# Cross attention: the maximum subtracted inside the transposed score product, the clip between product and exponential

## What is computed

```python
scale = D ** (-0.5)
q = (query @ Wq + bq).reshape(B, Nq, H, D).transpose(0, 2, 1, 3)
k = (key_value @ Wk + bk).reshape(B, Nkv, H, D).transpose(0, 2, 1, 3)
v = (key_value @ Wv + bv).reshape(B, Nkv, H, D).transpose(0, 2, 1, 3)
attn = jnp.einsum('bhqd,bhkd->bhqk', q, k) * scale
attn = jnp.clip(attn, -CLAMP, CLAMP)          # CLAMP = 10000
attn = jax.nn.softmax(attn, axis=-1)
attn = jnp.where(jnp.any(jnp.isnan(attn)), jnp.asarray(1.0 / Nkv, attn.dtype), attn)
x = jnp.einsum('bhqk,bhkd->bqhd', attn, v).reshape(B, Nq, Cq)
return x @ Wo + bo
```

## Time and profile before

| what | value |
|---|---|
| three runs | 860.56, 868.16, 869.66 us |
| median | 868.16 us |
| span of the profiled execution | 862.7 us |
| TensorE matmul busy | 727.4 us, 84% |
| VectorE busy | 639.6 us, 74% |
| ScalarE busy | 408.4 us, 47% |
| GpSimd busy | 198.2 us, 23% |
| mean granted TensorE clock | 0.931 of full speed |

### The profile page before, as it was taken

One profiled execution on the slowest core, in us unless ns is written; L12 is line 12 of the kernel. 1 busy time (PEld: TensorE's weight loads), 2 busy tenths in 40 slices (PEclk: granted clock), 3 DMA queues, 4 the chain that ended last, 5 costly groups with the idle time before them and its releaser, 6 DMA issues. The chain is left out here.

```text
span 862.7 us, 26300 instructions
## 1 busy us (share of the span) xinstructions
PE 727.4 (84%) x10112; PEld 545.5 (63%) x10112; DVE 639.6 (74%) x1802; ACT 408.4 (47%) x777; POOL 198.2 (23%) x317
## 2 busy tenths in 40 slices
PE   3468898888888889889999477887759999999997
PEld 2245565555556777667787245665547888888886
DVE  7568877787868989888996577887665766666653
ACT  3123223322235656656655365665635555554553
POOL 3333222232534212330200553342011110011100
PEclk9569989998898999999999599999998999999999
DMA  4000000140034221122200000000000000000000
GB/s 103 9 22 13 23 21 21 33 88 18 24 99 100 82 78 50 53 66 79 81 15 14 4 2 5 5 4 4 5 3 2 13 13 0 12 12 12 12 13 13
DMA packets 33082, 26.43 MB, mean 31 GB/s; under 512 B 9740, under 2 KB 29912, under 8 KB 32984
## 3 DMA queue, kind: packets, MB, share of 16 engines
q1 hardware_dynamic: 29944, 24.07, 10.5%
q10 hardware_dynamic: 3040, 0.98, 0.5%
HBM read 13.51 MB, written 7.34 MB: 24 GB/s over the span
## 5 line engine op out<-in xcount | busy, mean ns | idle before, releaser
L1931 PEld LDWEIGHTS bank<-w2r,hme 128*128 128x128 f32 x1024 | 132.2, 191 | 15.6 <-ACT hme L1876 1.4
L1931 PE MATMUL bank<-w2r,hme 128*128 128x128 f32 x1024 | 135.5, 276 | 0.0
L1876 ACT ACTIVATE hme<-bank,b 128x512 f32<-128x512 f32 x128 | 86.5, 687 | 96.3 <-PE bank L97 96.3
L984 ACT ACTIVATE P<-bank 128x512 f32<-128x512 f32 x128 | 76.6, 598 | 76.2 <-PE bank L1130 75.0
L1900 DVE SCALAR_TENSOR_TENSOR Xq<-bank,wgte,Xq 128x128 f32 (+1 forms) x256 | 72.1, 344 | 51.1 <-PE bank L1931 38.3
L1056 DVE TENSOR_SCALAR bank<-bank 128x512 f32<-128x512 f32 x128 | 89.6, 700 | 15.2 <-PE bank L1121 14.4
L1064 DVE TENSOR_REDUCE mx<-bank 128x4 f32<-128x512 f32 x128 | 87.1, 681 | 1.4 <-PE bank L1104 1.3
L500 ACT ACTIVATE w2r<-bank 128x512 f32<-128x512 f32 x40 | 23.9, 597 | 114.5 <-PE bank L814 82.8
L1130 PE MATMUL bank<-mT,negsel 128*128 128x128 f16 x512 | 51.0, 223 | 13.9 <-DVE bank L1056 12.6
L95 PE MATMUL bank<-xTe,w 128*128 (+1 forms) x128 | 48.8, 381 | 5.5 <-PEq L1295 5.5
L825 PE MATMUL bank<-w_raw,hm 128*128 128x128 f32 x320 | 50.3, 308 | 2.9 <-DVE X L739 2.8
(11 more groups left out here) (382 smaller groups left out, 1785.3 us busy)
## 6 DMA issues: line engine op xcount, KB each, us to landing
cross_q<-qh SPq DMA_DIRECT2D x24, 128.0 KB
Q<-cross_q SPq DMA_DIRECT2D x8, 384.0 KB, 3.9
X<-in_x SPq DMA_DIRECT2D x8, 256.0 KB, 2.8
Xq<-X SPq DMA_DIRECT2D x32, 64.0 KB
cross_k<-kh SPq DMA_DIRECT2D x16, 128.0 KB
Yq<-Y SPq DMA_DIRECT2D x32, 64.0 KB
out_x<-Xq SPq DMA_DIRECT2D x32, 64.0 KB, 1.7
cload<-in_ctx SPq DMA_DIRECT2D x8, 192.0 KB, 2.5
```

What stands on the lines that cost most here:

```text
L984: act.activation(P[j][:], TB[u % 3][:], ACT.Exp, scale=SCALE).then_inc(s["p_ready"], 1)
L1876: act.activation(hm[:, p % HR], UP[p % RING][:], ACT.Gelu_apprx_tanh, bias=b1[:, p:p + 1]).then_inc(s["gelu"], 1)
L1931: last = pe.matmul(Y[f % 2][:, cols], hm[:, p % HR, cols], w2r[:, p], start=(p % 2 == 0 and i == 0), stop=(p % 2 == 1), skip_group_check=True)
```

## The change

- `score` contracts over rows 0 to 95 only. Rows 96 to 127 of K hold -1 in row 96 + j of tile j (`negative_rows`: eight GpSimd instructions of 32 partitions by 2048 columns, four in layer 0 for the first buffer, four at the start of `attention1` for the second), and rows 96 to 127 of Q take the turned maxima, head by head. So `score_t`, over all 128 rows, gives the score less the maximum.
- `less_max`, `negsel` and `mT` are gone. The turn of the maxima (`turn_max`) is four transposes of 32 columns in place of one of 128; ScalarE's copy of the result has 32 partitions by 512 columns, in place of 128 by 128, and goes to Q.
- `score_t(b,0)` waits for that copy. All `score_t` and clips move one place back: group 3 of a batch is done in the next step. VectorE's preparation now follows clip(b,0).
- The clip stays in place in PSUM, on the difference, with other limits; the exponential takes a bias from a tile (`shift`), and follows the clip directly.
- On ScalarE the copy of the maxima goes ahead of exp(b-1,3).

```diff
+def negative_rows(pool, K, ident):
+    for j, t in enumerate(K):
+        last = pool.tensor_scalar(t[KEY_ROWS:128, :], ident[KEY_ROWS:128, KEY_ROWS + j:KEY_ROWS + j + 1].broadcast_to([32, 16 * S]),
+                                  -1.0, 0.0, ALU.mult, ALU.add)
+    return last
...
             def step(g):
                 for p in range(NBLK):
+                    if isinstance(g, int) and g == 0 and p == 1:
+                        pool.wait_ge(s["rsB"], 2)
+                        negative_rows(pool, c["K"][0], ident).then_inc(cs["neg_rows"], 1)
+                        pool.wait_ge(cs["neg_rows"], 1)
...
-                elif t == 4:
-                    dve.tensor_scalar(c["negsel"][:], ident[:, 0:NH].unsqueeze(2).broadcast_to([128, NH, 128]), -1.0, None,
-                                      ALU.mult)
...
+            pool.wait_ge(s["zeros"], 2)
+            negative_rows(pool, K[1], ident).then_inc(s["neg_rows"], 1)
+            pool.wait_ge(s["neg_rows"], 2)
...
-                act.wait_ge(s["t_neg"], u + 1)
+                act.wait_ge(s["t_clip"], u + 1)
                 after(act, s["o_psum"], u - 3)
-                act.activation(P[j][:], TB[u % 3][:], ACT.Exp, scale=SCALE).then_inc(s["p_ready"], 1)
+                act.activation(P[j][:], TB[u % 3][:], ACT.Exp, bias=c["shift"][:], scale=SCALE).then_inc(s["p_ready"], 1)
...
+                if has(b):
+                    act.wait_ge(s["mT_psum"], b + 1)
+                    q = Q[n % 2][KEY_ROWS:128, :].rearrange("r (h i q) -> r h i q", h=4, i=4)
+                    act.activation(q[:, :, i, :], M.rearrange("r (h q) -> r h q", h=4), ACT.Copy).then_inc(s["mT_ready"], 1)
                 if has(b - 1):
                     exp(b - 1, U - 1)
-                if has(b):
-                    act.wait_ge(s["mT_psum"], b + 1)
-                    after(act, s["t_neg"], U * b)
-                    act.activation(mT[:], M.bitcast(F16), ACT.Copy).then_inc(s["mT_ready"], 1)
...
             def step(b):
+                maxima(b + 1, 0)
+                clip(b - 1, 3)
+                maxima(b + 1, 1)
                 clip(b, 0)
-                maxima(b + 1, 0)
+                prepare(b // 4, b % 4)
+                maxima(b + 1, 2)
                 clip(b, 1)
-                maxima(b + 1, 1)
-                prepare(b // 4, b % 4)
-                clip(b, 2)
-                maxima(b + 1, 2)
-                clip(b, 3)
                 maxima(b + 1, 3)
...
+                clip(b, 2)
                 if has(b - 1):
...
             def score_t(b, j):
 
                 after(pe, s["p_ready"], U * b + j - 2)
+                if j == 0:
+                    pe.wait_ge(s["mT_ready"], b + 1)
+                    if b in (0, 4):
+                        pe.wait_ge(s["neg_rows"], 1 + b // 4)
...
-            def less_max(b, j):
-
-                pe.wait_ge(s["mT_ready"], b + 1)
-                pe.wait_ge(s["t_clip"], U * b + j + 1)
+            def turn_max(b):
+
+                pe.wait_ge(s["m_ready"], b + 1)
+                after(pe, s["mT_ready"], b)
                 for h in range(4):
-                    last = pe.matmul(TB[(U * b + j) % 3][:, cols(h)], negsel[:, 4 * j + h, :], mT[:],
-                                     start=False, stop=True, skip_group_check=True)
-                last.then_inc(s["t_neg"], 1)
+                    last = pe.transpose(M[:, cols(h)], m16[:, 32 * h:32 * h + 32], ident16[:])
+                last.then_inc(s["mT_psum"], 1)
...
                 if has(b):
-                    score_t(b, 0)
+                    turn_max(b)
                 if has(b - 1):
-                    less_max(b - 1, 3)
+                    score_t(b - 1, 3)
                 prepare(b // 4, b % 4)
...
-                    score_t(b, 1)
-                    less_max(b, 0)
+                    score_t(b, 0)
...
-                    score_t(b, 2)
-                    less_max(b, 1)
+                    score_t(b, 1)
...
-                    score_t(b, 3)
-                    less_max(b, 2)
+                    score_t(b, 2)
```

More of the change, by code:

```diff
@@ L30 @@
 NBLK = NE * 64 // C + 1
+KEY_ROWS = 96
+CLIP = 10000.0 * HD ** 0.5
+TOP = 28272.0
+TOP_GAP = CLIP - TOP
+FLOOR = -28080.0
+LEAST = -CLIP - FLOOR
 def after(eng, sem, value):
@@ L134, in cross_tiles @@
         "bo16": sb("bo16", [128, C], F16),
-        "negsel": sb("negsel", [128, NH, 128], F16),
+        "shift": sb("shift", [128, 1]),
         "st": sb("st1", [128, B, 6]), "mv": sb("mv1", [128, B, 2]), "rs": sb("rs1", [128, 2, B]),
@@ L436, in ahead @@
                 pool.memset(c["half"][:], -0.5)
+                pool.memset(c["shift"][:], -TOP_GAP * HD ** -0.5)
                 pool.memset(c["bo16"][:], 0.0).then_inc(cs["small_const"], 1)
@@ L564, in fill @@
                 elif p == 1:
-                    for t in c["K"][0] + c["Q"]:
+                    for t in c["K"][0]:
+                        dve.memset(t[0:KEY_ROWS].bitcast(mybir.dt.uint32), 0)
+                    for t in c["Q"]:
                         last = dve.memset(t[:].bitcast(mybir.dt.uint32), 0)
@@ L884, in attention1 @@
     SCALE = HD ** -0.5
-    CLIP = 10000.0 / SCALE
     RING = 4
@@ L892, in attention1 @@
         w1, ex = keep["w"], keep["expert"]
-        wv_c, bo16, negsel, Q, rT, lnbr = (c[n] for n in ("wv", "bo16", "negsel", "Q", "rT", "lnbr"))
+        wv_c, bo16, Q, rT, lnbr = (c[n] for n in ("wv", "bo16", "Q", "rT", "lnbr"))
         wo, bq_raw, w1r, lnb2 = (w1[n] for n in ("wo", "bq", "w1", "ln2_b"))
@@ L902, in attention1 @@
         m16 = sb("m16", [S, 128], F16)
-        mT = sb("mT", [128, S], F16)
         P = [sb(f"P{i}", [S, 4 * S]) for i in range(RING)]
@@ L914, in attention1 @@
         SB, TB = [S0, S1], [T0, T1, T2]
-        M = O[:, 2 * S:2 * S + S // 2]
+        M = O[0:32, 2 * S:4 * S].bitcast(F16)
         def has(b):
@@ L961, in _ @@
             for t in K[1]:
-                last = pool.memset(t[:].bitcast(mybir.dt.uint32), 0)
+                last = pool.memset(t[0:KEY_ROWS].bitcast(mybir.dt.uint32), 0)
             last.then_inc(s["zeros"], 1)
+            pool.wait_ge(s["zeros"], 2)
+            negative_rows(pool, K[1], ident).then_inc(s["neg_rows"], 1)
+            pool.wait_ge(s["neg_rows"], 2)
             def step(b):
@@ L1054, in clip @@
                 if has(b):
-                    dve.wait_ge(s["t_psum"], U * b + j + 1)
-                    dve.tensor_scalar(TB[(U * b + j) % 3][:], TB[(U * b + j) % 3][:], -CLIP, CLIP, ALU.max, ALU.min
-                                      ).then_inc(s["t_clip"], 1)
+                    u = U * b + j
+                    dve.wait_ge(s["t_psum"], u + 1)
+                    dve.tensor_scalar(TB[u % 3][:], TB[u % 3][:], LEAST, TOP_GAP, ALU.max, ALU.min).then_inc(s["t_clip"], 1)
             def maxima(b, j):
@@ L1079, in step @@
                     after(dve, s["mT_psum"], b + 1)
-                    dve.tensor_scalar(m16[:, 0:NH], mx[:], -CLIP, CLIP, ALU.max, ALU.min).then_inc(s["m_ready"], 1)
+                    dve.tensor_scalar(m16[:].rearrange("p (h r) -> p h r", h=4)[:, :, 0:U],
+                                      mx[:].rearrange("p (h j) -> p h j", j=U), FLOOR, TOP, ALU.max, ALU.min
+                                      ).then_inc(s["m_ready"], 1)
+                clip(b, 2)
                 if has(b - 1):
@@ L1103, in score @@
                 for h in range(4):
-                    last = pe.matmul(SB[j % 2][:, cols(h)], at(Q[b // 4 % 2], b, h), at(K[b // 4 % 2][j], b, h),
-                                     start=True, stop=True)
+                    last = pe.matmul(SB[j % 2][:, cols(h)], at(Q[b // 4 % 2], b, h)[0:KEY_ROWS],
+                                     at(K[b // 4 % 2][j], b, h)[0:KEY_ROWS], start=True, stop=True)
                 last.then_inc(s["s_psum"], 1)
@@ L1180, in step @@
                     bias(b % 4)
-                if has(b):
-                    pe.wait_ge(s["m_ready"], b + 1)
-                    after(pe, s["mT_ready"], b)
-                    pe.transpose(M.bitcast(F16), m16[:], ident16[:]).then_inc(s["mT_psum"], 1)
                 if has(b1):
```

8 lines of the change are left out of this document (4 added, 4 removed).

## The result

The changed kernel takes 932.97 us (median of four runs, 931.68 to 933.90) against 864.95 us (four runs too, the three of the table above and 861.75; 860.56 to 869.66) for the kernel before: ratio 1.078, interval 1.073 to 1.083. The forecast was 887 us. The sign was right, the size three times too small: +68 us, not +22. Two executions of later runs, 959.49 us of v4_behind and 3579.2 us of v7_bias, lie far above all others of their kernels and are left out of the medians and ratios.

What follows compares the result with a forecast made beforehand. TensorE and VectorE were both taken as near their limit. Cross-attention steps +17.2, tail +0.7 and clock +4.5 gave +22.4 us: 885.1 on the profiled span, 890.6 on the runs' median, taken as 887; range 868 to 906.

Steps and rivals of the forecast that it cites:

- What bounds the kernel: Cross attention: TensorE and VectorE both near their limit, with TensorE a little late for VectorE, often.
- the 5.49: Cross-attention step at VectorE's own pace: 7 x 0.60 + 0.71 + 0.58 = 5.49 us, the rest waiting for TensorE.
- Prices: Instruction times assumed: maxima copy 0.60 us, biased exponential 0.57 until the next, preparation 1.80, constant rows 3.1 each.
- the even case: Rival "About even": same chain but shorter, only the plain gains, +0 to +8 us, 866 to 876 us; chance 0.13.
- Now it starts at 0.58 + 4 x 0.60 = 2.98.: VectorE's clip(b,0) in each step: starts 2.98 us after the clamp m(b), before 0.58, with the maxima copy just hidden.
- the chain: Late exp(b,0) delays OT, y, score(b+1,3) and maximum 3, making a plain step 6.13 us, 5.64 before.
- Chunk starts: Steps i=0: VectorE's preparation waits for ScalarE's xh copy, 9.40 us per step, 8.15 to 9.65 before.
- The clock: Granted clock falls behind TensorE's 3.3 us idle stretch at chunk starts: three falls of 1.5 us, +4.5 us.
- GpSimd: Constant rows in layer 0 and attention: 3.1 us per instruction, 12.4 for four, hidden in idle time in both places.
- Tail: End of the cross attention: 0.7 us longer, from the same later exponential.
- VectorE at its own pace: Rival: y and subtraction don't hold back score(b+1,3), VectorE bounds the stage; -24.7 us, 838 us; chance 0.11.
- GpSimd is the slow one: Rival: constant rows cost 5.9 us an instruction, +11 in layer 0, 18 in all, 905 us; chance 0.11.

Runs made afterwards that it cites:

- v4_behind: v3_prep with score(b+1,2) placed directly behind score_t(b,0), ahead of the turn of On, projections and values; 866.76 us, ratio 1.0019.
- v7_bias: v4_ahead with Y copy before kh/qh copies, subtraction behind OE's turn, chunk 7 bias products before it, last score_t before values; 863.01 us, ratio 0.9966.
- v4_ahead: v3_prep with score(b+1,2) placed before score_t(b,0) on TensorE; 865.44 us, ratio 0.9987.
- e3_ot_y: Changed kernel with ScalarE's OT copy ahead of exp(b,0) and Y copy ahead of exp(b,1); 903.70 us.
- e4_proj: Changed kernel with TensorE's projections, V product and chunk 7 bias products moved behind the turn of On; 923.20 us.
- v3_prep: Changed kernel with constant rows behind xnB, OT and Y ahead of exponentials, projections and subtraction later, VectorE's preparation split; 877.14 us, ratio 1.011.

## Why the prediction was wrong, step by step

- **What bounds the kernel.** Right in that both engines were near their limit, so that added waits showed. But in plain steps the kernel before had no wait for TensorE worth the name: 5.65 us is VectorE's own length, as 5.64 in v4_ahead shows with the subtraction gone from TensorE, and the 5.49 was too low by 0.15. So TensorE's relief could buy little there from the start.
- **Prices.** The copy of the maxima: 0.58 us (0.60 taken). The exponential with a bias tile: 0.69 us, 0.57 to 0.58 until the next (0.57 taken). From the start of clip(b,0) to that of exp(b,0): 0.73 (0.80 taken). VectorE's preparation from 374.51 to 376.31: 1.80 as taken. Constant rows: 1.95 us each, not 3.1. None of this explains the miss. (In the range, the middle of the even case, 866 to 876, is 871, not 868; it changes nothing here.)
- **"Now it starts at 0.58 + 4 x 0.60 = 2.98."** This step failed. Measured 3.66 in a plain step and 3.73 in i=2 (353.33 to 357.06). I followed the later exponential into OT, y and score(b+1,3), and not into what stands behind it on ScalarE: the Y copy, which the turn of OE waits for, and the low parts, which the next projections wait for (0.47 us, at 355.38). Both stand ahead of scores for the next batch. From clip(b,0) on the chain was right: 3.17 (3.15) plain, and 4.08 (4.17) in i=2, 357.06 to 361.14. Over the 31 steps the first halves come to 136.1 us for 92.4 forecast, the second halves to 125.6 for 129.3: the whole miss of the stage, and 4 us more, lies in this one term. Y's part of it is shown by e3_ot_y (plain first half 2.97), the low part's by e4_proj (i=2 3.16). By kind of step, medians (i=0 to 3 over chunks 0 to 5):

| first half | plain | i=0 | i=1 | i=2 | i=3 |
|---|---|---|---|---|---|
| forecast | 2.98 | 2.98 | 2.98 | 2.98 | 2.98 |
| after | 3.66 | 3.78 | 6.5 | 3.73 | 3.85 |
| e3_ot_y | 2.97 | 3.64 | 4.2 | 3.73 | 3.85 |
| e4_proj | 3.66 | 3.84 | 5.4 | 3.16 | 3.3 |

- **Chunk starts.** 9.40 forecast, 11.5 to 12.1 measured from copy to copy. The step's second half is 6.27 us (9.40 - 2.98 = 6.42 forecast); what is missing stands behind it, in the first half of i=1, where 19 of the 43.7 us (136.1 less 92.4) lie. The rows in time of the kernel after:

```profile
373.87 0.61 ACT L225 ACTIVATE xh<-bank 128x512 f16<-128x512 f32 x1
...
377.61 0.69 ACT L1003 ACTIVATE P<-bank,shift 128x512 f32<-128x512 f32 x1 [3.13 <-DVE bank L1076]
378.19 0.27 ACT L1029 ACTIVATE Y<-bank 128x128 f32<-128x128 f32 x1
...
378.61 1.09 PE L1237 MATMUL bank<-ident,OE 128*128 128x128 f32 x4 [4.05 <-ACT Y L1029]
379.62 1.08 PE L1165 MATMUL bank<-P,V 128*32 128x128 f32 x16
```

The idle stretch that I had as 3.3 us is 4.05, and it ends at the turn of OE, not at the values: exp(b,1) waits for clip(b,1), which stands behind VectorE's preparation, and Y behind exp(b,1). VectorE's first half of i=1 behind it, from the clamp on, takes 6.2 us:

```profile
378.20 0.17 DVE L1098 TENSOR_SCALAR m<-mx 128x16 f16<-128x16 f32 x1
...
379.73 0.26 DVE L1106 RECIPROCAL dn<-bank 128x16 f32<-128x16 f32 x1 [0.76 <-PE bank L1237]
...
381.29 0.69 DVE L1083 TENSOR_REDUCE mx<-bank 128x4 f32<-128x512 f32 x1 [0.97 <-PE bank L1125]
...
383.77 0.69 DVE L1083 TENSOR_REDUCE mx<-bank 128x4 f32<-128x512 f32 x1 [0.70 <-PE bank L1125]
384.37 0.69 DVE L1076 TENSOR_SCALAR bank<-bank 128x512 f32<-128x512 f32 x1
```

- **The clock.** Falls were forecast in three of six chunk starts, at 1.5 us each; all six have one, with a mean granted clock of 0.67 to 0.79 over the step and 0.84 to 0.92 over the next. In this one the granted clock (last column but two) falls from 1.00 to 0.50, that is from 2.4 to 1.2 GHz:

```profile
374.00:376.00 2.00, 0.55 (x10) 0.38 (x7) 1.47 (x5) 0.48 (x1) 0.00 (x0) 1.00 0.36 111
376.00:378.00 2.00, 0.00 (x0) 0.00 (x0) 1.99 (x7) 0.39 (x1) 0.00 (x0) 0.61 0.62 202
378.00:380.00 2.00, 1.39 (x12) 1.08 (x16) 1.20 (x4) 1.15 (x3) 0.00 (x0) 0.50 0.04 10
380.00:382.00 2.00, 2.00 (x27) 1.21 (x20) 0.98 (x2) 0.18 (x1) 1.66 (x4) 0.50 0.08 23
```

The turn of OE takes 1.09 us there and 0.63 at full clock. The fall goes with the idle time ahead of it: idle stretches of 4.05 us had one in all four of chunks 1 to 4 here, 2.25 us in two or three of four in the profiles of before, 1.06 us in none of v3_prep. e3_ot_y, which removes the wait for Y and leaves 2.58 us, has 9.24 us in most chunk starts, near the 9.40 of the sum, but the fall comes in i=1 then (0.74 to 0.84). What the clock costs apart from the waits no run separates.

- **GpSimd.** Its own idle time hid the rows, as forecast (power at 80.80, still waiting 12.01 us for VectorE). The reading of the earlier trace rows failed. I took L597, a tensor_tensor that ran undisturbed beside a GpSimd tensor_tensor, as the judge of everything VectorE does beside the new instructions, and looked at the gate. What stood beside them was xnB, a tensor_scalar from SBUF to SBUF, and each of its instructions was held for about the length of one GpSimd instruction. The form of VectorE's instruction is not all of it: in the trace of before the same form, xnA, runs at its full pace (4 in 1.12 us) beside GpSimd's power for rsB, a tensor_tensor:
```profile
58.61 1.12 DVE L573 TENSOR_SCALAR xnA<-X,mvA,rsA 128x128 f32<-128x128 f32 x4
58.95 1.01 POOL L411 TENSOR_TENSOR rsB<-rsB,half 128x4 f32<-128x4 f32 x1
```

  Rows with another VectorE form, or with another GpSimd instruction, don't give the price of this pair, and before has no row of it. The Trainium skill, "SBUF — State Buffer", section "Who interferes with whom", says that VectorE's copy, cast and tensor_scalar can enter a mode that uses the port pair shared with GpSimd, and that the other engine is then blocked for a whole instruction. The 2.05 us against 0.34 agree, and the 1.12 us of xnA beside the power show no such block. I had cited that section for its other case, two SBUF inputs, and L597's 0.42 us show nothing of a wait there.
- **Tail.** +0.7 forecast, +3.8 measured. The wait for Y is there too, and the granted clock over the tail was 0.71, against 0.87 in before; e3_ot_y, with Y ahead, has +1.0 at a clock of 0.92, v7_bias +1.7 at 0.87. The parts of Y and of the clock are not told apart.
- **Rivals.** "VectorE at its own pace" was dismissed because ScalarE's order is unchanged. That was right for the change as made, and the repaired order does reach that pace (5.64, forecast 5.49), but only after seven moves, and it is the pace of before. "GpSimd is the slow one" was wrong in the price, and right that layer 0 would pay, though by another way. No rival had a second chain through the same late exponential.

## What to carry to other kernels

When a change makes one instruction late on an in-order engine, list everything that stands behind it on that engine, and for each who waits for it; the first chain found is not the only one, and here the one not followed (the Y copy, the turn of OE, the next scores) cost more than the one that was. Removing work from an engine is worth only what other engines were waiting for it: here plain steps had VectorE's length already, and the same change was +68 us with the old order of the side work and -3 us once that was redone. When a kernel has to be reordered to carry a change, run the new order on the old kernel too; without that the gain can't be shared out. When GpSimd work is put into idle time, look at the very pairs of VectorE and GpSimd instructions that will run side by side, not at one convenient neighbour.
